# State 14 of the scan summed in columns, and the last step's sums re-placed, in a gated Mamba and mixture-of-experts block

## What is computed

```
x = x + tanh(g_xattn) * ssm(ctx, layernorm(x))
x = x + tanh(g_ffn) * ffn(layernorm(x))

ssm:  x = in_proj_w @ ctx ; u = silu(conv(x) + conv_b)       512 channels, 4 taps
      dt, B, C = x_proj_w @ u ; delta = softplus(dt_proj_w @ dt + b)
      for each of 16 states n:
          st_n[l] = exp(delta[l]*A_n) * st_n[l-1] + delta[l]*u[l]*B_n[l]
      y = sum over n of C_n * st_n  + D*u ; y = y * silu(z)
ffn:  a shared expert plus 7 routed experts (top 3 of a softmax, weights normalised),
      each silu(x @ W1) * (x @ Wg) @ W2, 512 wide
```

## Time and profile before

| what | us |
|---|---|
| median of three runs | 1370.07 |
| the profiled execution's own time | 1370.06 |
| its span in the profile | 1368.3 |
| TensorE busy with matmuls | 1313.6 (96%) |
| VectorE busy | 967.9 (71%) |
| ScalarE busy | 623.3 (46%) |
| POOL busy | 572.6 (42%) |

### The profile page before, as it was taken

The page is one execution under the profiler, slowest core; times in us unless marked ns, Lnnn a source line. Parts: engine busy times, 40 slices in busy tenths (PEclk is TensorE's granted clock), DMA queues, the critical chain, the costliest instruction groups (busy, mean ns, idle before and its releaser), DMA issues.

```text
span 1368.3 us, 17588 instructions
## 1 busy us (share of the span) xinstructions
PE 1313.6 (96%) x6018; PEld 1036.5 (76%) x6018; DVE 967.9 (71%) x1074; ACT 623.3 (46%) x1016; POOL 572.6 (42%) x317
## 2 busy tenths in 40 slices
PE   7899799999999999999999899999999899999999
PEld 4455478777777778888888778888888788888887
DVE  6899867899999776699999666699999523211111
ACT  6888366666565345544444135554443121111111
POOL 0000545788898421566765111566674211111111
PEclk8999999999999999999999999999999999999999
DMA  6211676776667755655555756555555665555552
GB/s 222 93 54 62 208 286 245 270 262 236 225 245 268 284 202 196 197 189 184 173 187 187 276 186 202 201 194 189 168 194 160 210 214 186 184 184 184 184 187 89
DMA packets 92301, 269.16 MB, mean 197 GB/s; under 512 B 11633, under 2 KB 11761, under 8 KB 91841
## 3 DMA queue, kind: packets, MB, share of 16 engines
q1 hardware_dynamic: 86912, 261.01, 55.7%
q10 hardware_dynamic: 5312, 7.16, 1.5%
HBM read 210.20 MB, written 57.93 MB: 196 GB/s over the span
## 4 chain that ended last, share of the span: by engine, by line
PE 76%; DVE 15%; issue 6%; ACT 2%; DMA 0%; DVEq 0%; ACTq 0%; POOL 0%
PE ps_hg L526 24%; PE ps_h L526 21%; PE ps_y L526 15%; DVE st L1278 8%; PE ps_y L707 8%; PE ps_mid L605 4%; DVE st L1269 2%; DVE y_rows L1289 2%; PE ps_mid L567 1%; PE ps_mid L526 1%; PE ps_y L549 1%; ACT dA L932 0%; DVE acc L1435 0%; DMA in_w<-in_in_wT_dram 0%; PE ps_mid L582 0%
## 5 line engine op out<-in xcount | busy, mean ns | idle before, releaser
L1597 POOL TENSOR_TENSOR h_lo<-h_tmp,h_hi 128x512 fp32r<-128x512 f32 x128 | 238.0, 1863 | 520.5 <-ACT h_hi L1007 458.2
L526 PE MATMUL ps_h<-x_hi,w_split 128*128 128x512 f32 x1024 | 344.9, 399 | 1.6 <-ACT x_hi L969 0.9
L526 PE MATMUL ps_hg<-x_hi,wg_split 128*128 128x512 f32 x1024 | 342.2, 395 | 0.6 <-DVE h_tmp L1442 0.6
L1278 DVE TENSOR_TENSOR_SCAN st<-dA,st 128x1024 f32<-128x1024 f32 x128 | 325.0, 2549 | 0.0
L1442 DVE TENSOR_TENSOR h_tmp<-h_tmp,ps_hg 128x512 f32<-128x512 f32 x128 | 88.1, 688 | 283.9 <-PE ps_hg L526 281.4
L526 PE MATMUL ps_y<-w_split,h_hi 128*128 128x512 f32 x1024 | 254.5, 396 | 0.0
L1007 ACT ACTIVATE h_hi<-h_tmp 128x512 fp32r<-128x512 f32 x128 | 80.6, 630 | 328.7 <-DVE h_tmp L1442 328.7
L526 PEld LDWEIGHTS ps_h<-x_hi,w_split 128*128 128x128 f32 x1024 | 193.2, 189 | 42.8 <-issue 2.9
L526 PEld LDWEIGHTS ps_hg<-x_hi,wg_split 128*128 128x128 f32 x1024 | 192.4, 188 | 40.4 <-issue 1.0
L526 PEld LDWEIGHTS ps_y<-w_split,h_hi 128*128 128x128 f32 x1024 | 188.1, 188 | 37.6
L1001 ACT ACTIVATE h_tmp<-ps_h 128x512 f32<-128x512 f32 x128 | 76.2, 595 | 293.2 <-PE ps_h L526 291.7
(11 more groups left out here) (161 smaller groups left out, 1298.6 us busy)
## 6 DMA issues: line engine op xcount, KB each, us to landing
w_split<-split_scratch SPq DMA_DIRECT2D x192, 512.0 KB, 5.5
wg_split<-split_scratch SPq DMA_DIRECT2D x96, 512.0 KB, 4.6
split_scratch<-w_split SPq DMA_DIRECT2D x64, 512.0 KB, 4.5
b_all<-xd_scratch SPq DMA_DIRECT2D x64, 256.0 KB, 4.1
split_scratch<-wg_split SPq DMA_DIRECT2D x32, 512.0 KB, 3.0
w_raw<-in_W_dram SPq DMA_DIRECT2D x14, 1024.0 KB, 7.4
wg_raw<-in_Wg_dram SPq DMA_DIRECT2D x7, 1024.0 KB, 9.4
dA<-in_x_dram SPq DMA_DIRECT2D x4, 1024.0 KB, 8.5
```

The source lines that it names most:

```text
L526: mm = pe.matmul(out_, lhs[a], rhs[c], start=first and q == 0, stop=last and q == len(sides) - 1)
L1278: dve.tensor_tensor_scan(flat[1], flat[0], flat[1], 0.0, ALU.mult, ALU.add).then_inc(scan_done, 1)
L1597: pool.tensor_tensor(h_lo[:, j, :], h_tmp[j % 2][:], h_hi[:, j, :].bitcast(F32), ALU.subtract).then_inc(hl_ready, 1)
```

## The change

State 14 joins `COLS` in turns 2 and 3, so six states are summed in columns and ten in rows. POOL takes it in front of step 7's first `h_lo`. State 15's block i is now summed in the place in which it is turned (p = i for i = 0 to 3). The blocks of `y_cols` are turned in places 4 and 5, two in each, behind state 15's four, and VectorE adds them there and makes y of the same two blocks. Turn 1 and batch 3's steps are as they were.

```diff
-        COLS = list(range(0, DS - 1, 3))
+        COLS = list(range(0, DS - 1, 3)) + [DS - 2]
...
         def sum_place(m, n, i):
             if not late(m):
                 return len(front_names(m)) + T * n + i
-            return len(front_names(m)) + T * ROWS.index(n) + (2 * i if n == DS - 1 else i)
+            return len(front_names(m)) + T * ROWS.index(n) + i
 
         def cols_place(m, i):
 
-            return sum_place(m, DS - 1, i) + 1
+            return sum_place(m, DS - 1, i) + T
...
                     n = first + g // T
                     if 0 <= n < DS:
                         state_to_rows(m, n, g % T)
-                        if late(m) and n == DS - 1:
-                            columns_to_rows(m, g % T)
+                    if late(m) and first == DS - 1 and g in (T, T + 1):
+                        columns_to_rows(m, 2 * (g - T))
+                        columns_to_rows(m, 2 * (g - T) + 1)
...
                 if r == 0:
                     if n >= 2:
                         sum_rows(m, n - 2, T - 1)
-                        if late(m) and n - 2 == DS - 1:
-                            add_columns(m, T - 1)
                 elif 1 <= n <= DS:
                     sum_rows(m, n - 1, r - 1)
-                    if late(m) and n == DS:
-                        add_columns(m, r - 1)
...
                 def last(p):
-                    slot(m, DS + p // T, p % T) if p <= T else None
+                    if late(m):
+                        if p < T:
+                            sum_rows(m, DS - 1, p)
+                        if p in (T, T + 1):
+                            add_columns(m, 2 * (p - T))
+                            add_columns(m, 2 * (p - T) + 1)
+                    elif p <= T:
+                        slot(m, DS + p // T, p % T)
...
                     for e in range(2, NE):
                         step_(STEPS * b + e, ahead=lambda j: column_state(m, e - 2, 2 * j) if j < 2 else None)
+                    for part in (0, 2):
+                        column_state(m, NC - 1, part)
                 step_(STEPS * b + NE)
```

## The result

| | before | changed |
|---|---|---|
| median, us | 1370.24 (1369.11 to 1371.49, 4 runs) | 1358.95 (1358.26 to 1360.79, 4 runs) |
| profiled execution's own time, us | 1370.06 | 1358.72 |
| its span, us | 1368.3 | 1356.9 |

The ratio is 0.9919, with a 95% interval of 0.9902 to 0.9937. That is 11.3 us faster; 10.0 was forecast, inside the range of 1357.5 to 1364.5.

The account below looks back on a forecast made before the run. TensorE was taken to set the pace, standing idle where it waits for VectorE to read a bank. Gains of 0.6 + 4.4 = 5.0 us a turn, 10.0 for turns 2 and 3, gave 1360.1 us; range 1357.5 to 1364.5.

Parts of the forecast that it names:

- The wait that was read: Step 7, turn 2, behind gate(0) and gate(1): TensorE's column block waits for VectorE's read behind the h-multiply, 1.87 us idle.
- State 15's first block: Step 7: TensorE turns it at 755.6 instead of 756.20, a gain of 0.6 us.
- three sums out, three waits of about 0.6 in: VectorE around state 15: state 14's sums leave, waits for POOL enter; last scan ends at 755.5 instead of 755.6.
- The stretch to gate(3): From state 15's first block to gate(3)'s end, no bank is waited for: 27.45 becomes 23.07, gain 4.4 us.
- the 773: Predicted sign: in step 7 of turn 2 turned column blocks stand as eight matmuls at about 768.7 and 773.
- Places 4 and 5: VectorE's adds, y, residual and statistics fit: done at 778.5, gate(3) ending at 778.7; up to 1.1 late in the bad case.
- The cover of 7 us: State 14's last POOL add ends at 761.5, the columns' turning that waits for it comes at 768.65: nothing on the path.
- A: Rival, more collisions: all four port-sharing operations of state 15 wait a whole POOL operation; gain 2.1 a turn, 1365.9; chance 0.12.
- B: Rival, no collisions: last scan ends at 753.7, then up(0) binds; gain 6.0 a turn, 1358.1; chance 0.08.
- C: Rival, POOL at its slowest: all eight operations at 3.26 us, columns turned 2.6 late; gain 2.4 a turn, 1365.3; chance 0.07.
- D: Rival, slower: POOL operations at 4.1 us make state 14 9.2 late, 1378.5; loss starts beyond 5.0 late; chance 0.03.
- E: Rival: the gaps stay, the banks' wait moves to places 4 and 5, losing the 4.4; 1368.9; chance 0.04.

Follow-up runs that it names:

- experiment 1: The kernel before, with only state 15's sums and the column adds moved to the place of turning in turns 2 and 3; 1362.60 us, ratio 0.9926.
- Experiment 5: The changed kernel, with POOL starting state 14 only when state 15's last scan is done; 1357.50 us, ratio 0.9903.
- experiment 2: The changed kernel without its state 14 part, so columns turned in places 4 and 5 and sums in the place of turning; 1361.02 us, ratio 0.9915.
- experiment 4: The changed kernel with state 15's sums one place behind again (places 1 to 4); 1359.26 us, ratio 0.9905.
- +4: The changed kernel with four more POOL multiplies of 128x512 a turn between the halves of state 14; 1359.09 us, ratio 0.9915.
- experiment 8: The changed kernel with six more POOL multiplies of 128x512 a turn between the halves of state 14; 1361.70 us, ratio 0.9933.
- experiment 7: The changed kernel with eight more POOL multiplies of 128x512 a turn between the halves of state 14; 1371.17 us, ratio 0.9999.
- experiment 3: The kernel before with state 14 in columns on POOL and nothing else changed; 1385.75 us, ratio 1.0094.

## Why the prediction was right

**The wait that was read.** The prediction took TensorE's losses behind gate(0) and gate(1) as waits of the column block: state 15's block ends at 760.9, and the column block is 1.87 us late. The chain skips the row of state 15's block, and TensorE's timeline shows it otherwise (experiment 1): that block itself starts only at 761.96, after 1.51 us of waiting for the sum of the block before. The loss was 1.87 all the same, and its cause, a sum that stands behind the h-multiply, was as the prediction had it, so the forecast's sum was not hurt.

**State 15's first block.** Up(0) of step 7 was forecast 1.5 earlier and came 1.48 earlier from the reference scan. The block was forecast 0.6 earlier and came 1.13 earlier. The direction was right and a size off: the term "three sums out, three waits of about 0.6 in". The sums were 1.95 as put, but the waits came to 0.45 + 0.40 + 0.45 = 1.30. If the scan of 2.72 at 746.50 spends its last 2.27 working, it starts to work at 746.95, and a POOL multiply of 1.28 that ends there began at 745.67, a quarter of a microsecond ahead of the end of the multiply row in front of it (744.30 + 1.62 = 745.92). I had let it begin at the row's end. By the forecast's own times its waits were 0.66, 0.65 and 0.55; the measured ones are 0.21, 0.25 and 0.10 shorter, together the 0.55 by which I was short. The hand-over is worked out, not seen: POOL's rows stand two to a line. Experiment 5 confirms the mechanism: without POOL the three operations take 2.27, 1.21 and 2.27.

**The stretch to gate(3).** Forecast 4.4, measured 27.45 - 23.02 = 4.43. Experiment 1 gives 4.18 with the place of the sums alone, experiment 2 gives 4.49 with both moves and without state 14. The reason that the prediction gave, that block i is read in place i, is not needed in the changed kernel: experiment 4 reads it one place later and waits for nobody. Each of the two moves suffices. The columns were forecast at 768.7 and 773 and turned at 767.91 and 771.52; the 773 did not follow from the forecast's own terms, which give 772.3.

**Places 4 and 5.** Forecast done 0.2 ahead of gate(3)'s end; measured done as it ended. VectorE's third and fourth h-multiply started 0.1 us behind their gates' ends; making y in place 5 met POOL (2.14 instead of 1.41), and the residual took 1.28. Nothing reached TensorE.

**POOL.** Forecast 745.1 to 761.5, measured 744.8 to 760.8. The cover of 7 us was 7.1 (767.9), and experiments 6 to 8 find its edge: +4 costs nothing, +6 costs 1.2 to 1.6 a turn, +8 costs 6.1.

**The rivals.** A and B were the two sides of the collisions. The measured gain of 5.56 lies between the forecast's 5.0 and B's 6.0; experiment 5 is B, and 0.5 a turn is what it had left. C did not come: the mean of POOL's operations stayed at 2.03 and 2.08. D did not happen, but its price was wrong: it counted the wait alone, and in experiments 3 and 7 waits of 5.2 and 4.0 us were followed by half of TensorE's clock. The point from which POOL's lateness makes the kernel no faster is a wait of about 4 us (experiment 7), not the 5.0 that I gave. The Trainium skill's rule against elementwise work on GpSimd (GPSIMD Engine Reference, Engine selection) holds for the engine's time (a two-input operation of 128x512 takes 1.28 us alone on POOL, two take 1.28 together on VectorE) and not for the kernel's: four sums of 0.73 became eight operations of 2.05 on the mean, on an engine that nobody waited for. E was excluded: no wait stands in front of L614.

**The sum.** 2 x 5.56 = 11.1 against 10.0 forecast; the profiled executions differ by 11.3, of which 0.24 was there before turn 2's changed stretch.

**State 14 is worth about 1 us a turn.** That is the timelines' 1.07 (experiment 2); the medians, 1361.02 to 1358.95, agree but were not taken side by side, and by the ratios they are within the noise. Alone it costs 7 a turn (experiment 3), since the column sum is then late for place 0. State 14 together with experiment 1's places was not run; its column block would stand in place 0 as well.

## What to carry to other kernels

When a producer waits for a bank, look at where the consumer's instruction stands in its queue and not only at how long it takes: here a read of 0.7 us that stood behind the wrong operation cost 1.87 us, twice a turn, and moving it brought most of the gain with no work removed. Work moved to an idle engine is free up to a point that can be worked out and then tested by adding dummy work; where two engines exclude each other, start it when the other's part of the critical chain is over. And price a new wait on TensorE twice: 1.3 us was paid once, 4.0 and 5.2 us also in the clock behind them, and in the kernel with the wait of 5.2 us so were two waits of 1.5 us that had cost only themselves in the kernel before.

## What the hardware showed beyond that

- Waits of TensorE of 1.3 us (experiment 8) and 1.51 us (before) left the granted clock at 1.00. Waits of 4.0 and 5.2 us (experiments 7 and 3) were followed by a clock of 0.50 to 0.52, and two matmuls of 128x512 took 1.05 instead of 0.63 us. In experiment 3 two of four waits of 1.51 us were followed by 0.50 too.
- VectorE's scan or two-input multiply and POOL's two-input operations took turns: 2.72 and 1.61 us for VectorE's beside POOL against 2.27 and 1.21 alone, and 2.75 for POOL's against 1.28 alone. The hand-over, as worked out above, lies about 0.25 us ahead of the end of the VectorE row.
